# Attention block on one core: matmuls on idle banks at the start, three banks for turned tiles, scores issued inside the value matmuls

## The reference

```
q, k, v = x @ Wq.T, x @ Wk.T, x @ Wv.T           # 16 heads of 32
scores  = where(mask, -inf, q k^T * 32**-0.5)
out     = softmax(scores) @ v, heads joined, @ Wo.T
xn      = out / rms(out) * rms_scale * (1 + sc) + shift    # sc, shift from silu(cond) @ Wc.T + bc
x1      = x + xn
result  = x1 + rotation(x1)                       # 4x4 quaternion products with cond and q_right, gate
```

## Time and profile before

| | |
|---|---|
| median of three runs | 875.37 us (875.3 to 876.35) |
| profiled execution, its own time | 876.17 us |
| its span | 874.4 us |
| TensorE matmul busy | 856.1 us (98%) |
| VectorE, ScalarE, GpSimd busy | 628.4, 621.4, 481.7 us |

### The profile page before, as it was taken

How to read it: one execution, slowest core, us unless ns; L and a number is a source line. 1 busy time by engine, 2 the same in 40 slices (tenths; PEclk the granted TensorE clock), 3 DMA queues, 4 the chain that set the end, 5 groups by cost and what they waited for, 6 DMA issues and landing times.

```text
span 874.4 us, 17160 instructions
## 1 busy us (share of the span) xinstructions
PE 856.1 (98%) x5334; PEld 638.5 (73%) x5334; DVE 628.4 (72%) x1516; ACT 621.4 (71%) x1505; POOL 481.7 (55%) x346
## 2 busy tenths in 40 slices
PE   6999999999999999999999999999999999999997
PEld 4878888888887665777677776777677776777674
DVE  4612212213316888999999999999999999999986
ACT  5322332332326889999999999999999999999882
POOL 0999990000000111277757776677757776677894
PEclk9999999999999999999999999999999999999999
DMA  8854554654596785577785778578766777669201
GB/s 273 333 180 182 208 191 178 212 191 173 175 296 228 164 192 116 134 196 161 157 207 127 165 183 207 121 170 208 156 169 170 161 163 197 155 144 233 83 26 49
DMA packets 82306, 153.75 MB, mean 176 GB/s; under 512 B 8472, under 2 KB 9112, under 8 KB 82224
## 3 DMA queue, kind: packets, MB, share of 16 engines
q1 hardware_dynamic: 82224, 152.75, 64.7%
HBM read 102.35 MB, written 50.36 MB: 175 GB/s over the span
## 4 chain that ended last, share of the span: by engine, by line
PE 95%; DVE 2%; issue 1%; DMA 1%; ACT 1%; SPq 0%; POOL 0%; DVEq 0%; ACTq 0%
PE banks L685 26%; PE banks L108 13%; PE banks L714 13%; PE banks L731 10%; PE banks L389 10%; PE banks L390 10%; PE banks L391 10%; PE banks L695 2%; DVE turned_probs L775 1%; DMA raw<-in_xT 1%; DVE probs L117 1%; DVE probs L590 0%; PE banks L425 0%; ACT turned_probs L876 0%; DVE banks L821 0%
## 5 line engine op out<-in xcount | busy, mean ns | idle before, releaser
L125 ACT ACTIVATE probs<-probs,least 128x512 f32<-128x512 f32 x512 | 363.4, 714 | 0.0
L117 DVE CUSTOM_DVE_ANT_0 probs<-banks,mask_bias 128x512 f32<-128x512 f32 x512 | 331.7, 680 | 31.4 <-PE banks L108 31.4
L685 PE MATMUL banks<-ident,probs 128*128 128x128 f32 x2048 | 308.6, 273 | 4.2 <-DVE turned_probs L775 1.9
L685 PEld LDWEIGHTS banks<-ident,probs 128*128 128x128 f32 x2048 | 245.5, 140 | 75.7 <-issue 15.9
L108 PE MATMUL banks<-k_rows,q_rows 128*128 128x512 f32 x496 | 236.2, 478 | 0.0
L775 DVE COPY turned_probs<-banks 128x512 f32<-128x512 f32 x256 | 175.6, 686 | 9.8 <-PE banks L685 9.7
L876 ACT ACTIVATE turned_probs<-banks 128x512 f32<-128x512 f32 x256 | 151.1, 590 | 34.8 <-PE banks L685 31.8
L328 DVE SCALAR_TENSOR_TENSOR late<-banks,late 128x512 fp32r<-128x512 f32 x64 | 44.1, 690 | 174.6 <-ACT late L294 174.6
L590 POOL TENSOR_TENSOR late<-rot,late 128x2048 f32<-128x2048 f32 x28 | 128.9, 4602 | 0.6 <-DVE late L808 0.6
L294 ACT ACTIVATE late<-banks 128x512 fp32r<-128x512 f32 x64 | 38.3, 598 | 120.1 <-PE banks L391 117.8
L714 PE MATMUL banks<-turned_probs,v_sb 128*32 128x512 f32 (+1 forms) x1088 | 116.9, 570 | 1.0 <-ACT turned_probs L876 1.0
(11 more groups left out here) (112 smaller groups left out, 1260.9 us busy)
## 6 DMA issues: line engine op xcount, KB each, us to landing
q_rows<-q_scratch SPq DMA_DIRECT2D x128, 256.0 KB, 6.0
k_rows<-k_scratch SPq DMA_DIRECT2D x124, 256.0 KB, 6.9
q_scratch<-late SPq DMA_DIRECT2D x64, 256.0 KB, 2.3
k_scratch<-late SPq DMA_DIRECT2D x64, 256.0 KB, 2.3
v_scratch<-v_out SPq DMA_DIRECT2D x32, 256.0 KB, 2.1
v_sb<-v_scratch SPq DMA_DIRECT2D x8, 1024.0 KB, 11.8
out<-late SPq DMA_DIRECT2D x29, 256.0 KB, 5.8
raw<-in_xT SPq DMA_DIRECT2D x7, 1024.0 KB, 5.7
```

The source lines that it names most:

```text
L117: dve.tensor_tensor_reduce(self.probs[:, n % RING, :], self.ps[:, n % 4, :], self.mask_bias[:, c, :], 1.0, 3e38, ALU.add, ALU.min, self.le ...
L125: act.activation(self.probs[:, n % RING, :], self.probs[:, n % RING, :], ACT.Exp, bias=self.least[:, n % 32:n % 32 + 1], scale=-1.0, accum ...
L685: last = pe.transpose(turn_ps[:, at % 2, j * P:(j + 1) * P], probs[:, n % RING, j * P:(j + 1) * P], ident[:, :])
```

## The change

It has four parts. (1) At the start, ten matmuls whose result nobody reads run on bank 7 while the first inputs arrive. The four value tasks of the first batch are made together, slice by slice and way by way, in four banks, and the first slice of `x` is loaded from ScalarE's queue. Wq is loaded and split in four slices, Wk is split after the value copies. (2) Turned tiles have three banks (0, 1, 4) and scores three (5 to 7), so a score waits for the mask three back. (3) The first four units get tables of their own (`early`), and which engine copies a tile out is a table too (`BY_ACT`). (4) `values` is called in four parts, and in the 29 goes that fall into groups of kind `early` (3) or `whole` (26) one score is issued between two parts (`GO_SCORES`).

```diff
-SCORE_AHEAD, MASK_AHEAD, EXP_AHEAD = 9, 6, 1
+SCORE_AHEAD, MASK_AHEAD, EXP_AHEAD = 7, 5, 2
+SCORE_BANKS, TURN_BANKS = 3, 3
+KIND = ["early"] * NG + ["whole"] * (U - 2 - NG) + ["half"] * 4
-MASKS = {16: (0, 3, 1, 1, 2, 0, 2, 0, 1, 1, 1, 0, 2, 0, 1, 1), 8: (0, 2, 2, 2, 1, 0, 0, 1)}
-EXPS = {16: (0, 6, 0, 1, 1, 0, 2, 0, 2, 0, 1, 1, 1, 1, 0, 0), 8: (0, 2, 1, 1, 2, 1, 0, 1)}
+SCORES = {'early': (1, 2, 1, 0, 0, 1, 1, 1, 1, 2, 0, 1, 0, 1, 2, 1), 'whole': (1, 2, 0, 1, 1, 0, 1, 2, 0, 1, 1, 1, 0, 2, 1, 1), 'half': (1, 1, 1, 1, 1, 1, 1, 1)}
+GO_SCORES = {'early': (0, 1, 0, 0), 'whole': (1, 0, 0, 0), 'half': (0, 0, 0, 0)}
+MASKS = {'early': (1, 0, 1, 1, 0, 4, 0, 1, 2, 2, 0, 0, 2, 0, 2, 0), 'whole': (3, 0, 2, 0, 0, 3, 1, 1, 0, 1, 1, 1, 1, 1, 1, 0), 'half': (0, 2, 2, 2, 1, 1, 0, 0)}
+EXPS = {'early': (0, 5, 2, 1, 0, 1, 0, 1, 0, 1, 1, 1, 1, 1, 1, 0), 'whole': (0, 5, 1, 1, 0, 0, 2, 0, 2, 1, 0, 0, 3, 1, 0, 0), 'half': (0, 2, 1, 1, 1, 2, 0, 1)}
+BY_ACT = {'early': '0111011010011001', 'whole': '0101010110010101', 'half': '01010011'}
-PROJECT_AT = {m: [(m + NG, at) for at in (2, 3, 4, 5, 6, 7, 9, 9, 11, 12, 13, 14)] for m in range(CHUNKS - 3)}
+PROJECT_AT = {m: [(m + NG, at) for at in (3, 4, 4, 6, 7, 7, 9, 10, 10, 13, 13, 13)] for m in range(CHUNKS - 3)}
+WARM = 10
...
-        if n >= 4:
-            pe.wait_ge(self.masked, n - 3)
+        if n >= SCORE_BANKS:
+            pe.wait_ge(self.masked, n - SCORE_BANKS + 1)
...
+            def warm():
+                pe.wait_ge(warm_set, 1)
+                for _ in range(WARM):
+                    last = pe.matmul(banks[:, 7, :], mask_bias[:, 0, 0:P], mask_bias[:, 0, :], start=True, stop=True)
+                last.then_inc(warmed, 1)
+            def first_values():
+                for k in range(KC):
+                    for way, hi_count, lo_count in ((0, 2, 0), (1, 2, 1), (2, 2, 2)) if k < KC - 1 else ():
+                        pe.wait_ge(first_hi, 2 * k + hi_count)
+                        if lo_count:
+                            pe.wait_ge(first_lo, 2 * k + lo_count)
+                        for c in range(VT):
+                            x_part, w_part = x_lo if way == 2 else x_hi, w_lo if way == 1 else w_hi
+                            pe.matmul(proj[:, c, :], x_part[:, 0, k, c * P:(c + 1) * P], w_part[2][:, k, :],
+                                      start=(k == 0 and way == 0), stop=False)
...
-        turn_ps, value_ps, y_ps, score_ps = banks[:, 0:2, :], banks[:, 2, :], banks[:, 3, :], banks[:, 4:8, :]
+        turn_ps, value_ps, y_ps = [banks[:, j, :] for j in (0, 1, 4)], banks[:, 2, :], banks[:, 3, :]
+        late_ps = banks[:, 5:8, :]
...
+            def more_scores(first, count):
+                for n in range(first, first + count):
+                    if EARLY_END <= n < N:
+                        scores.score(pe, n)
+                return first + count
+            made = SCORE_AHEAD
             for n, (v, u, i, c) in enumerate(ORDER):
                 t = n - FIRST[v]
-                if t == VALUES_AT[SIZE[v]] and v > 0:
-                    values(v - 1)
+                if t == VALUES_AT[KIND[v]] and v > 0:
+                    for part in range(TC):
+                        values(v - 1, part)
+                        made = more_scores(made, GO_SCORES[KIND[v]][part])
                     turn_scale(v - 1)
-                if n + SCORE_AHEAD < N:
-                    scores.score(pe, n + SCORE_AHEAD)
+                made = more_scores(made, SCORES[KIND[v]][t])
```

More of the change, by code:

```diff
@@ L383, in _, with passes @@
         def _(pe):
-            def passes(out, hi, lo, other_hi, other_lo, first=False):
-                for k in range(KC):
-                    if first:
-                        pe.wait_ge(first_lo, 2 * k + 2)
+            def warm():
[4 more added lines that the diff above has]
+            def first_values():
+                for k in range(KC):
+                    for way, hi_count, lo_count in ((0, 2, 0), (1, 2, 1), (2, 2, 2)) if k < KC - 1 else ():
[6 more added lines that the diff above has]
+                                      start=(k == 0 and way == 0), stop=False)
+                pe.wait_ge(first_lo, 2 * KC)
+                for c in range(VT):
+                    t = slice(c * P, (c + 1) * P)
+                    pe.matmul(proj[:, c, :], x_hi[:, 0, KC - 1, t], w_hi[2][:, KC - 1, :], start=False, stop=False)
+                    pe.matmul(proj[:, c, :], x_hi[:, 0, KC - 1, t], w_lo[2][:, KC - 1, :], start=False, stop=False)
+                    pe.matmul(proj[:, c, :], x_lo[:, 0, KC - 1, t], w_hi[2][:, KC - 1, :], start=False,
+                              stop=True).then_inc(projected, 1)
+            def passes(out, hi, lo, other_hi, other_lo, second=False):
+                for k in range(KC):
+                    if second:
+                        pe.wait_ge(second_lo, k + 1)
                     pe.matmul(out, hi(k), other_hi(k), start=(k == 0), stop=False)
@@ L394, in batch @@
             def batch(b, p, first=False, last=False):
-                for c in range(VT):
-                    if c == 0 and not first:
+                if first:
+                    first_values()
+                for c in range(VT) if not first else ():
+                    if c == 0:
                         pe.wait_ge(x_lo_ready, b)
-                    if not first:
-                        pe.wait_ge(qk_lo_ready, QKT * b - 4 + c + 1)
+                    pe.wait_ge(qk_lo_ready, QKT * b - 4 + c + 1)
                     t = slice(c * P, (c + 1) * P)
                     passes(proj[:, c, :], lambda k: x_hi[:, p, k, t], lambda k: x_lo[:, p, k, t],
-                           lambda k: w_hi[2][:, k, :], lambda k: w_lo[2][:, k, :],
-                           first=first and c == 0)
+                           lambda k: w_hi[2][:, k, :], lambda k: w_lo[2][:, k, :])
                 for m in range(QKT):
@@ L746, in _ @@
                 turn(n)
-            values(V - 1)
+            for part in range(TC):
+                values(V - 1, part)
             turn_scale(V - 1)
@@ L755, in _ @@
                 for k in range(4):
-                    last = pe.matmul(score_ps[:, (j + 3) % 4, :], ident[:, :], late_mix[j][:, k, :],
+                    last = pe.matmul(turn_ps[j], ident[:, :], late_mix[j][:, k, :],
                                      start=(k == 0), stop=(k == 3))
@@ L833, in _ @@
                 t = n - FIRST[v]
-                if t == INVERT_AT[SIZE[v]] and v > 0:
+                if t == INVERT_AT[KIND[v]] and v > 0:
                     invert(v - 1)
-                for _ in range(MASKS[SIZE[v]][t]):
+                for _ in range(MASKS[KIND[v]][t]):
                     if EARLY_END <= masks < N:
@@ L922, in _ @@
                 t = n - FIRST[v]
-                for _ in range(EXPS[SIZE[v]][t]):
+                for _ in range(EXPS[KIND[v]][t]):
                     if EARLY_END <= exps < N:
@@ L1056, in program @@
         banks = ctx.enter_context(nc.psum_tensor("banks", [P, 8, 512], F32))
-        scores = Scores(nc, ctx, rows, mask_bias, probs, banks[:, 4:8, :])
+        scores = Scores(nc, ctx, rows, mask_bias, probs, banks[:, 8 - SCORE_BANKS:8, :])
         projected, qk_lo_ready, mod_stored = [ctx.enter_context(nc.semaphore(n))
```

149 lines of the change are left out of this document (88 added, 61 removed).

## The result

The changed kernel takes 877.74 us (median of 14 executions, 875.2 to 878.97), the one before 875.34 on the same chips (14 executions, 874.25 to 877.42). The medians are 2.4 us apart. The ratio, estimated from all executions, is 1.0022 with a 95% interval of 1.0012 to 1.0032, so it is slower by 0.2%. The forecast was 874.2, a little faster: the time is inside its range, but it moved the other way.

The account below looks back on a forecast made before the run. The prediction took TensorE to bound the kernel (95% of the chain). Its terms, -2.9 + 1.3 - 0.8 - 2.1 + 4.2 - 0.9 = -1.2, took 875.4 to 874.2 us; range 871.5 to 877, chance 0.50.

Parts of the forecast that it names:

- start: First batch: value tasks end 4.9 us earlier, but TensorE then waits for VectorE, so the gain is 2.9 us.
- early scores: After task 4: the fourth score waits for the first mask, so task 5 begins 1.3 us late.
- unit 1: First turn to first go: VectorE copies fewer tiles and three banks loosen the turns, 0.8 us gained.
- units 2 to 4: Early units without projection matmuls: 17.2 us each, 0.7 less than before, 2.1 us gained in all.
- whole units: 26 units: third bank saves 0.17, width changes cost 0.33, so TensorE sets 18.05 us each; 4.2 us lost.
- half groups: Last groups: three turns wait for a bank; three banks take 0.9 us off, despite a later last mask.
- attention in sum: All terms after the start, from early scores to half groups: together a loss of 1.7 us.
- the fourth score bank is missed: Rival, whole units: VectorE's hole over 1.26 us decides; at 1.5 a unit lasts 18.3, 880.7 us in all; chance 0.22.
- the widths change for free: Rival, whole units: switching stationary width in the go costs nothing, -3.4 instead of +4.2, 866.6 us; chance 0.13.
- The start is not held by VectorE: Rival: small inputs land 2 us earlier, another 2 gained, 872.2 us; chance 0.15 shared with more in the early part.
- The pause: Before the first key task (m = 4): TensorE must stand still about two us until VectorE finishes `qk_lo` of task 0.
- The idle matmuls: At the start: ten matmuls in idle time cost nothing and decide almost nothing, since VectorE imposes about 30.5 anyway.

Follow-up runs that it names:

- a2: Kernel before with only the new first batch, attention as before: 872.96 us, ratio 0.9983; its first bunch is eight faster executions, median 872.6.
- a3: Changed kernel's attention behind the first batch of the kernel before: 879.74 us, ratio 1.0053.
- b2: Kernel before with the new first batch, VectorE making `qk_lo` of tasks 0 and 1 before mask and silu work; attention as before: 871.02 us.
- c4: b2 plus, in the first four units, a third turned-tile bank, the change's `BY_ACT` row and a score in the go: 869.02 us, ratio 0.9929.
- c2: b1 with a second score put into each whole-unit go, taken from those behind it: 883.29 us, ratio 1.0091 to the kernel before.
- c1: b1 with undivided goes in the whole units, the score behind them: 874.03 us, ratio 0.9985 to the kernel before.
- b1: Changed kernel with VectorE making `qk_lo` of tasks 0 and 1 before the mask and silu work: 874.33 us, ratio 0.9988 to the kernel before.
- b4: Changed kernel with GpSimd waiting until VectorE's first mask instruction is done: 877.82 us, ratio 1.0024 to the kernel before.
- b3: Changed kernel with eight more idle matmuls on bank 7 ahead of TensorE's wait before the first key task: 876.58 us, ratio 1.0024.
- c3: Changed kernel with the edits of b3 and b4 together: 876.22 us, ratio 1.0018 to the kernel before.
- a1: Changed kernel timed again without any edit: 876.68 us, ratio 1.0015 to the kernel before.
- a4: Changed kernel without the ten idle matmuls at the start: 879.7 us, ratio 1.005 to the kernel before.

## Why the prediction was wrong

The terms are read off the goes of the two profiled executions. "Before" is the earlier trace rows and the goes at 292.05, 345.71 and 811.07; "after" has them at 287.79, 338.74 and 809.51. The first early score is at 266.69 before and 262.57 after, task 5 at 267.60 and 265.07.

| term | predicted | measured |
|---|---|---|
| start, up to the first early score (trace) | -2.9 | -4.12 |
| start alone (a2, medians; first bunch) | -2.9 | -2.25; -2.6 |
| early scores, to task 5 | +1.3 | +1.59 |
| unit 1, from task 5 to its go | -0.8 | -1.73 |
| units 2 to 4 | -2.1 | -2.71 |
| whole units | +4.2 | +5.41 |
| half groups and end | -0.9 | +0.56 |
| attention in sum | +1.7 | +3.1 (trace), +3.3 to +4.5 (runs) |

**The start in the trace is larger than in the medians.** The difference of 4.12 holds about 1.5 us that a3 shows to be the late fall of the step in the trace of before. What is left, 2.6, is what a2's first bunch gives.

**The attention part was 1.4 us too low in the sum, by the traces, and 1.6 to 2.8 by the runs.** This alone turns the sign: -1.2 and 1.4 is +0.2, and a3 shows the part by itself. The step that failed worst is "Half groups": "With three banks I take 0.9 us off". The gain was put on banks alone, and VectorE's new list took it back. From the last but one group's go to the next it is 11.19 us after (832.73 to 843.92) and 10.38 before. Before, the chain there was TensorE but for one copy of 0.69; after, it runs through VectorE from 835.31 to 841.55, over masks, the residual (L882) and copies:

```profile
832.73 1.93 PE banks L775 x32
...
835.49 0.69 DVE probs L129
...
837.76 0.54 DVE late L882
...
838.71 0.68 DVE turned_probs L849
...
840.94 0.61 DVE turned_probs L849
841.55 0.14 issue
841.69 0.63 PE banks L747 x4
...
843.92 1.86 PE banks L775 x32
```

No run undoes the list of the half groups alone. But in the kernels that have the old attention at this place (a2, b2, c4) this group takes 10.3 to 10.4, and 11.1 to 11.7 in all others. The prediction had named a later mask as a risk and let the gain win. The second is the size of the whole units: 18.11 and not 18.05, over 26 units, 1.2 us. TensorE pays 0.39 for the split (0.33 was taken) less 0.17 for the bank. The early scores cost 0.3 more than taken: the fourth score starts where it was expected, 2.0 behind the first, but behind the stop task 5 follows it by 0.50 in the chain and not by 0.23. Against these stand unit 1 and units 2 to 4, which gained 1.5 more than was taken.

**The mechanism of the whole units was half right.** The price of a change of width holds: 0.33 taken, 0.39 in the trace, 0.35 in c2. But the split is not alone in setting the unit. VectorE's hole is 1.39 in the changed kernel and 1.40 in c1, where 1.2 to 1.3 and 1.5 were computed. The rival "the fourth score bank is missed" was said to decide from 1.26 on, and it does: VectorE's 16.7 plus 1.39 is as long as TensorE's list. So undoing the split alone gives nothing, as c1 shows; with both undone, in c4, the unit is back at 17.90. That "the widths change for free" (-8.8) is excluded by c2. "The start is not held by VectorE" was put at 2 us more, by inputs that land earlier; b1 and b2 made it so by another order, and it gave 2.35 and 1.9 (872.96 less 871.02 is 1.94).

**The pause was priced at its own length.** The prediction found it, with its place, its cause and its length ("must stand still for about two": 1.65 to 2.18 in four traces), and then took the clock behind it for granted. b4's trace shows 1.6 us lost after such a pause. That it is the same in the changed kernel's eight longer executions with a low clock is an inference. A mean clock of 0.998 proves little by itself: executions of the kernel before have it too, at 875.2 to 876.0 us, and b1 has it without any pause. But 0.997 and less stands in 15 of the 53 executions of the kernels with the open pause and in 2 of the 22 with a filled one (b3 and c3). It stands in none of the 40 of the variants without a pause, and in none of the 71 of before that were timed beside them. It carries a part of the loss, not all: in c3 the key task waits as long, without any low clock, and it has 876.22, while the changed kernel has 876.68 and 877.74 in its two series. So the clock is worth some 0.5 to 1.5 us of the median, an estimate from medians of different sets. With a1's 876.68 and b1's 874.33, the pause in all costs 2.35, of which its length is 1.9 (c3 less b1).

**The idle matmuls.** "If the step should not fall early, the end moves from 28.2 to about 30.5, which is what VectorE imposes anyway" looked at TensorE alone. a4 shows what it missed: VectorE's own list moves too, it then loses the race to GpSimd's instruction, and the pause gets longer instead of vanishing.

Taken together: -1.2 forecast, +1.4 for the attention terms, +0.3 for the start in the first bunch, is +0.5, which is where the first bunch of five lies (median 876.01, +0.7). The falls of the clock, and what moves executions at the full clock, bring the median to +2.4; in the second series, a1, it is +1.5. The falls are not needed for the wrong sign: c3 has none and is 0.9 us over before. Right were the start within 0.3 in the first bunch, the pause, the direction of the early scores, of the early units and of the whole units, and the gain in units 2 to 4, whose bounds (0 to 3.6) hold 2.7. The errors partly cancel: the half groups and the whole units missed by 2.7 together, and the early units by 1.5 the other way.

What stays open: why c3 has four executions of 11 at 877.1 to 877.9 with the full clock (a1 and the changed kernel have some like them). None of them was profiled. The traces hold two things that move an execution at the full clock. In the six traces of kernels with the pause and the idle matmuls the mask instruction starts between 21.60 and 22.51, with the landing, and the key task moves with it. And single units are longer than their neighbours: 18.40 once in a3, 18.22 once in c3, 18.25 and 18.23 in b2, where the others are 18.1 and 17.9. The second goes far to explain why a3 gives more than 3.1: in its trace the attention costs about 4.0 once the 1.5 of the start is taken out, and 0.3 of that is its one long unit and 0.5 its half group of 11.6. Up to the 4.5 of the medians it stays open.

## What to carry to other kernels

A pause of TensorE has two prices, its length and what the clock may do behind it; shorten what comes ahead of a wait only together with the list of the engine waited for (here the same instructions of VectorE in another order were worth 2.35 us). Before a term is put on a freed bank or a freed wait, read which engine's list comes next there, and compute work plus hole for each: in the steady units and in the last groups it was VectorE both times. And where executions spread, one profile shows one of them; look where it lies among the times before its rows are taken for the kernel.

## What the runs showed of the hardware

- Behind pauses of the same length, 2.17 and 2.18 us, TensorE's clock once stayed at 1.00 and once fell to 0.66 in the next 5 us.
- VectorE's conversion of 128x2048 from uint8 to bf16 takes 1.23 us when it starts first and 3.77 when GpSimd's 128x1536 multiplication has begun 0.73 before it. Each time that it starts behind GpSimd's it ends about 1.1 after it (a4, b1, b2, c4). GpSimd's takes 3.80 when VectorE's is 0.04 ahead, and 2.75 when it is made to wait for it.
- Mean granted clocks of 0.997 and less stand in 15 of 53 executions of kernels with such a pause, and in none of 111 without it.
- With the same first batch, the step of 512 columns fell from 0.43 to 0.23 near 15.3 us in one trace and near 12.5 in another, behind unbroken matmuls since 9.11 and 8.91. It moved the rest by 1.5 us.
- A score with a stationary operand of 128 columns inside matmuls of 32 columns costs 0.35 to 0.39 us more than its own 0.24.
